# Attention passes of a graph network: each tile of neighbours gathered once, into 16 places, and copied from there step by step

## What is computed

```
# first: two GraphSAGE layers
agg = segment_sum(h[src], dst) * inv_deg          # mean over the incoming edges
h   = concatenate([h, agg]) @ W + b               # 128 -> 256, relu, 256 -> 128, log_softmax
# second: two attention layers (4 heads of 32)
k_j   = k[src] + e;  alpha = einsum(q[dst], k_j) / sqrt(32)      # e = edge weight * We
ex    = exp(alpha - segment_max(alpha, dst)[dst])
a     = ex / segment_sum(ex, dst)[dst]
out   = segment_sum((v[src] + e) * a, dst)
h     = relu(batchnorm(beta * x_r + (1 - beta) * out)) + h_res
```

## Time and profile before

| | us |
|---|---|
| median of 3 runs (8920.58 to 8937.23) | 8926.18 |
| profiled execution, its own time | 8917.18 |
| its span, first to last instruction | 8915.1 |
| first pass, first to last gather | 124.7 to 2075.7 |
| first attention pass, first to last gather | 4280.3 to 6377.2 |
| second attention pass, first to last gather | 6609.8 to 8705.1 |

### The profile page before, as it was taken

One profiled execution on the slowest core, in us unless ns is written; L12 is line 12 of the kernel. 1 busy time (PEld: TensorE's weight loads), 2 busy tenths in 40 slices (PEclk: granted clock), 3 DMA queues, 4 the chain that ended last, 5 costly groups with the idle time before them and its releaser, 6 DMA issues. The chain is left out here.

```text
span 8915.1 us, 117136 instructions
## 1 busy us (share of the span) xinstructions
PE 5021.9 (56%) x23604; PEld 4287.5 (48%) x23604; DVE 3720.9 (42%) x10693; ACT 3012.8 (34%) x10976; POOL 6457.3 (72%) x6755
## 2 busy tenths in 40 slices
PE   1444444446555555554666656666666666666666
PEld 1443443445444444443555555555455555555553
DVE  4000000003000000004677777777787777777778
ACT  4444444443433333333322222222222222222222
POOL 4777777773777777776677777777657777777776
PEclk7556556557555555556777777777787777777777
DMA  5333333336444444445666676766547667766663
GB/s 164 120 121 121 119 118 115 121 119 199 128 123 121 121 126 121 121 139 154 208 216 217 216 217 215 218 215 217 173 156 217 214 217 216 218 215 219 214 219 108
DMA packets 698550, 1514.21 MB, mean 170 GB/s; under 512 B 190785, under 2 KB 399706, under 8 KB 677966
## 3 DMA queue, kind: packets, MB, share of 16 engines
q0 software_dynamic: 258752, 639.99, 24.6%
q10 hardware_dynamic: 161312, 487.14, 15.8%
q1 hardware_dynamic: 277870, 380.19, 14.1%
HBM read 1294.45 MB, written 212.31 MB: 169 GB/s over the span
## 5 line engine op out<-in xcount | busy, mean ns | idle before, releaser
L1695 POOL DMA_INDIRECT conv_kv<-key_value,conv_src x3320 | 3183.3, 959 | 1100.0 <-issue 988.5
L881 POOL DMA_INDIRECT second_msg<-sage_hidden_projected,second_src x1516 | 1430.3, 943 | 585.4 <-issue 459.3
L881 POOL DMA_INDIRECT first_msg<-sage_in,first_src x1564 | 1475.6, 943 | 501.3 <-issue 476.1
L1933 PE MATMUL conv_ps_sums<-conv_kv,conv_sel 128*128 128x136 f32 x6640 | 1326.1, 352 | 584.4 <-DVE sums L1845 537.0
L2012 ACT ACTIVATE conv_selT<-conv_place,minus_partition 128x512 f32<-128x512 f32 x830 | 599.1, 722 | 2766.2 <-DVE conv_qwe L1737 2688.3
L1933 PEld LDWEIGHTS conv_ps_sums<-conv_kv,conv_sel 128*128 128x128 f32 x6640 | 1140.8, 246 | 729.2 <-DVE sums L1845 550.5
L1918 PE MATMUL conv_ps_query<-query_table,conv_selT 128*128 x6640 | 1245.4, 346 | 347.1 <-ACT conv_selT L2017 232.5
L1083 PE MATMUL first_ps_sums<-first_msg,first_sel 128*128 x3328 | 823.3, 431 | 1025.0 <-ACTq L951 994.9
L1918 PEld LDWEIGHTS conv_ps_query<-query_table,conv_selT 128*128 128x128 f32 x6640 | 1093.5, 246 | 436.5 <-issue 433.9
L1083 PE MATMUL second_ps_sums<-second_msg,second_sel 128*128 x3328 | 827.2, 429 | 786.7 <-ACTq L951 786.7
L1083 PEld LDWEIGHTS first_ps_sums<-first_msg,first_sel 128*128 128x128 f32 x3328 | 725.0, 322 | 1132.9 <-issue 1132.9
(11 more groups left out here) (271 smaller groups left out, 4229.8 us busy)
## 6 DMA issues: line engine op xcount, KB each, us to landing
conv_place<-place_rows SPq DMA_DIRECT2D x416, 512.0 KB
conv_sel<-selections ACTq DMA_DIRECT2D x414, 512.0 KB, 5.8
selections<-first_sel ACTq DMA_DIRECT2D x52, 2048.0 KB, 7.0
second_sel<-selections ACTq DMA_DIRECT2D x104, 1024.0 KB, 5.1
conv_kv<-key_value,conv_src POOLq DMA_INDIRECT x3320, 3.6
first_msg<-sage_in,first_src POOLq DMA_INDIRECT x1564, 2.5
second_msg<-sage_hidden_projected,second_src POOLq DMA_INDIRECT x1516
conv_pen<-run_penalties SPq DMA_DIRECT2D x416, 48.5 KB
```

Of the source, the lines that this page charges most:

```text
L881: pool.indirect_dma_start(msg[:, to * MW:to * MW + D], None, table, bass.IndirectOffsetOnAxis(ap=src[:, lap % 2, j:j + 1], axis=0)).then_i ...
L1695: pool.indirect_dma_start(kv[:, h * CH + j, :], None, t.kv_d, bass.IndirectOffsetOnAxis(ap=src[:, h, j:j + 1], axis=0)).then_inc(gathered[ ...
L1933: last = pe.matmul(sums_of(h, step), sel[:, k % SELG, step % GR, :], kv[:, h * CH + step, DEN:2 * D], start=True, stop=True)
```

## The change

- An attention pass gathers each tile once (391 groups of four), into `held`, a ring of 16 places. ScalarE copies a step's rows from there to the step's place in `kv` (56 places now), from an address in a register: for every half chunk it reads 16 places from a list, for every group the number of tile groups needed. VectorE waits for the copy (`copied`).
- SP loads the sources straight from the input, turns landed gathers into `tiles_in`, and frees a tile group (`held_free`) when the copies of its last step are done, two groups behind. All its other loads move to ScalarE's queue.
- The first pass also turns each selection: TensorE transposes it, ScalarE copies it out of PSUM (`keep_turned`) and a DMA of 256 KB a group stores it. The attention passes load turned selections two groups at a time; Abs, Relu and the broadcast rows go.
- Setup writes the two new lists and no longer the turned sources and place rows. The first own loads of both GraphSAGE passes are issued at the start of the pass (`begin`). The attention pass is unrolled on GpSimd and ScalarE, where it was a loop over pairs of chunks.

```
+HELD = 16
+HELD_GROUPS = HELD // GR
+LATE = 2
+PLACES = 56
+PLACE_GROUPS = PLACES // GR
...
 # first pass, ScalarE
+                def keep_turned(c, k):
+                    n = c * KG + k
+                    act.wait_ge(sel_turned, n + 1)
+                    if n >= 2:
+                        act.wait_ge(selT_out[n % 2], 16 * (n // 2))
+                    act.activation(selT[:, n % 2, :], psS[:, n % 2, :], ACT.Copy).then_inc(selT_taken, 1)
+                    act.wait_ge(selT_taken, n + 1)
+                    act.dma_start(t.selT_d[c, :, k * GR * P:(k + 1) * GR * P], selT[:, n % 2, :]).then_inc(selT_out[n % 2], 16)
...
                         release(n, h, g, k)
                         following(n + 1, 1 - h, g + h, k, used)
+                        if keeps and n + k > 0:
+                            keep_turned(*divmod(n * KG + k - 1, KG))
...
 # first pass, TensorE, behind the sums of each group
+                            for i in range(GR):
+                                last = pe.transpose(psS[:, n % 2, P * i:P * i + P], sel[:, h * CH + k * GR + i, :], t.ident[:, :])
+                            last.then_inc(sel_turned, 1)
...
 # attention pass, SP
+                def landed(g):
+                    sp.wait_ge(gathered[g % HELD_GROUPS], 16 * GR * (g // HELD_GROUPS) + 16 * GR)
+                    sp.sem_inc(tiles_in, 1)
+
+                def release(g):
+                    last = sp.value_load(lastuse[0:1, g:g + 1], min_val=1, max_val=STEPS // GR)
+                    sp.wait_ge(copied, last)
+                    sp.sem_inc(held_free, 1)
...
+                for g in range(GROUPS):
+                    landed(g)
+                    if g % KG == KG - 1 and (g // KG + 2) * CH < TILES:
+                        load_src(g // KG + 2)
+                    if g >= LATE and g - LATE + HELD_GROUPS < GROUPS:
+                        release(g - LATE)
...
 # attention pass, GpSimd
+                for g in range(GROUPS):
+                    lap, k = divmod(g, KG)
+                    if k == 0:
+                        pool.wait_ge(src_in[lap % 2], 16 * (lap // 2) + 16)
+                    if g >= HELD_GROUPS:
+                        pool.wait_ge(held_free, g - HELD_GROUPS + 1)
+                    pool.sem_inc(go_p, 1)
+                    for i in range(GR):
+                        j = k * GR + i
+                        pool.indirect_dma_start(
+                            held[:, (g * GR + i) % HELD, :], None, t.kv_d,
+                            bass.IndirectOffsetOnAxis(ap=src[:, lap % 2, j:j + 1], axis=0)).then_inc(gathered[g % HELD_GROUPS], 16)
...
 # VectorE
-                    dve.wait_ge(gathered[h * KG + k], 16 * GR * g + 16 * GR)
+                    dve.wait_ge(copied, KG * c + k + 1)
...
-                    mine = kv[:, h * CH:h * CH + CH, :]
-                    dve.tensor_copy(mine[:, :, DEN:DEN + HEADS], p)
+                    for lo, hi in runs_of(c):
+                        at_place = place_of_step(c * CH + lo)
+                        mine = kv[:, at_place:at_place + hi - lo, :]
+                        dve.tensor_copy(mine[:, :, DEN:DEN + HEADS], p[:, lo:hi, :])
...
 # ScalarE
+                def select_turned(a, q):
+                    c, h, g = a
+                    lo, hi = 2 * q, min(2 * q + 2, groups(a))
+                    half = q % (SELG // 2)
+                    act.wait_ge(q_ready, KG * c + 2 * q + SELG - 2)
+                    act.dma_start(selT[:, 2 * half:2 * half + hi - lo, :].rearrange("p k w -> p (k w)"),
...
+                def weights(c):
+                    act.wait_ge(wd_used, c + 1)
+                    act.dma_start(wd[:, c % 2, :, :], t.edge_d[:, 1:3, c * CH:c * CH + CH]).then_inc(wd_in[c % 2], 16)
+
+                def records(c):
+                    h = c % 2
+                    act.wait_ge(blk_used, c + 1)
...
+                def copy(a, k):
+                    c, h, g = a
+                    n = KG * c + k
+                    if k == 0:
+                        act.wait_ge(list_in[h], 16 * g + 16)
+                    if k % (KG // 2) == 0:
+                        regs = [act.alloc_register(f"{tag}_held{n}_{i}") for i in range(CH // 2)]
+                        act.load(regs, lists[0:1, h, k * GR:k * GR + CH // 2])
+                        from_tiles[:] = [act.snap(r, donate=True, min_val=0, max_val=HELD - 1) for r in regs]
+                    tiles = act.value_load(lists[0:1, h, CH + k:CH + k + 1], min_val=1, max_val=GROUPS)
+                    act.wait_ge(tiles_in, tiles)
+                    if n >= PLACE_GROUPS:
+                        act.wait_ge(sums_ready, 2 * KP + 2 * (n - PLACE_GROUPS) + 2)
+                    for i in range(GR):
+                        j = k * GR + i
+                        last = act.activation(kv[:, place_of_step(c * CH + j), :],
+                                              held[:, bass.ds(from_tiles[j % (CH // 2)], 1), :].rearrange("p a d -> p (a d)"), ACT.Copy)
+                    last.then_inc(copied, 1)
...
                     select(b, 0)
                     select(b, 1)
                     if a is not None:
-                        select_turned(a, 2)
+                        select_turned(a, 1)
+                        copy(a, 0)
                     act.wait_ge(drop_ready, c + 1)
                     act.activation(fac[:, :], drop[:, :], ACT.Exp).then_inc(fac_exp, 1)
                     act.wait_ge(below_ready, c + 1)
                     act.activation(expo[:, :], below[:, :], ACT.Exp).then_inc(expo_ready, 1)
                     if a is not None:
-                        for k in range(3, 6):
-                            select_turned(a, k)
+                        select_turned(a, 2)
+                        copy(a, 1)
+                        copy(a, 2)
+                        copy(a, 3)
+                    if after is not None:
+                        weights(after)
+                    if a is not None:
+                        select_turned(a, 3)
                     select(b, 2)
                     if a is not None:
-                        select_turned(a, 6)
+                        copy(a, 4)
+                        copy(a, 5)
                     select(b, 3)
+                    if after is not None:
+                        lists_of(after)
+                        records(after)
+                    if a is not None:
+                        copy(a, 6)
+                    if following is not None:
+                        select_turned(following, 0)
                     if a is not None and groups(a) == KG:
-                        select_turned(a, 7)
+                        copy(a, 7)
```

More of the change, by code:

```diff
@@ L256, in setup_phase @@
         bank = sb("bank", [SJ, P], I32)
+        held = sb("held", [SJ, P], I32)
         ring_f = sb("ring_f", [SJ, P])
@@ L688, in tensor, with begin @@
             last.then_inc(self.made, 1)
+    def begin(self, act):
+        self.load(act, (0, 0, 0))
+        self.load(act, (1, 1, 0))
+        act.wait_ge(self.w_in, 32)
     def load(self, act, turn):
@@ L766, in scalar @@
         n, h, g = turn
-        if isinstance(n, int) and n == 0:
-            self.load(act, (0, 0, 0))
-            self.load(act, (1, 1, 0))
         if not (isinstance(n, int) and n >= SPANS):
@@ L802, in sage_edges @@
         lastuse = sb("lastuse", [1, GROUPS], I32)
+        selT = sb("selT", [P, 2, GR * P]) if keeps else None
+        psS = psum("ps_sel", [P, 2, 512]) if keeps else None
+        sel_turned, selT_taken = sem("sel_turned"), sem("selT_taken")
+        selT_out = [sem(f"selT_out{b}") for b in range(2)]
         ps = psum("ps_sums", [P, SUM_BANKS * 512])
@@ L999, in pair @@
                         chunk(n, h, g, n - 1 if n > 0 else None)
+                own.begin(act)
                 if keeps:
@@ L1585, in slots_of, with place_of_step, runs_of, conv_edges @@
     return slots + [(last, ADDS[last - NEAR], CH, (PAIRS_OF[last - NEAR][0], KP))]
-def conv_edges(nc, t, tag):
+def place_of_step(step):
+    return step % PLACES
+def runs_of(c):
+    lo = place_of_step(c * CH)
+    return ((0, CH),) if lo + CH <= PLACES else ((0, PLACES - lo), (PLACES - lo, CH))
+def conv_edges(nc, t, src_cols, tag):
     with room(nc, tag) as (sb, psum, sem):
         HR = HEADS * CH
-        kv = sb("kv", [P, RING, 2 * D])
+        kv = sb("kv", [P, PLACES, 2 * D])
+        held = sb("held", [P, HELD, 2 * D])
+        lists = sb("lists", [1, 2, CH + KG], I32)
+        lastuse = sb("lastuse", [1, GROUPS], I32)
         sel = sb("sel", [P, SELG, GR, P])
         selT = sb("selT", [P, SELG, GR * P])
-        place = sb("place", [P, 2, 2 * GR * P])
         src = sb("src", [P, 2, CH], I32)
@@ L1685, in _ @@
             @block.gpsimd
             def _(pool):
-                def gathers(a):
-                    c, h, g = a
-                    pool.wait_ge(src_in[h], 16 * g + 16)
-                    for k in range(groups(a)):
```

(52 more changed lines are left out.)

132 lines of the change are left out of this document (57 added, 75 removed).

## The result

Median after the change 8872.33 us, beside 8921.71 for the kernel before in the same session: ratio 0.9944 [0.9933, 0.9956]. That is 49 us saved, where 171 were forecast. The profiled execution took 8870.64 us (span 8868.6) against 8917.18.

A forecast was written before the change was run, and what follows sets the result against it. POOL's gathers were taken to set the pace of all 104 stages. Stages 180 us saved, minus 7 for pass ends, minus 4 for the first pass's end, plus 2 for setup, made 171: median 8755 us, range 8680 to 8880.

The forecast's parts named there:

- The sixteen held places: Ring between POOL's gathers and ScalarE's copies: POOL can run on with 2.6 us in hand; 38.7 us a stage, 180 saved.
- the term of 0.3 for the coupling: Attention stage: loops of 38.1 and 38.4 us, so close, cost each other 0.3 us, giving 38.7.
- Landing: Held ring: a group is landed 3 x 1.25 + 3.6 = 7.4 us after its first gather starts.
- SP's serial release: SP frees a tile group behind the landing two groups later: 7.4 + 1.4 us, under POOL's 10.0.
- The copies' spread: ScalarE's copies against an even 4.75 us a group: offsets 3.6 to 0.4, spread 3.2, 2.6 us in hand.
- The ring is too short: Rival at `held_free`: POOL stops once a stage for up to 5.0 us; 43.1 a stage, 9200 us; chance 0.12.
- Gathers removed: POOL, attention passes: 1564 gathers instead of 1660 at 1.25 us, so 38.1 us a stage; that floor would give 242 us.
- Size of the copies: ScalarE, per group: four 128x256 copies replace Abs and Relu; 420 ns each, 1.4 us for four (bounds 1.28 and 2.5).
- The sixteen register reads: ScalarE, before the copies of groups 0 and 4: reading sixteen registers and a tile count takes 1.8 us.
- Group 0: VectorE waits 0.7 us for ScalarE's first copy of a stage (bounds 0 and 1.5).
- Group 1: VectorE waits 0.9 us for ScalarE's copy behind the exponential of `below` (bounds 0.3 and 1.5).
- Group 4: VectorE waits 0.7 us on average for ScalarE's copy, behind `select(b, 2)` and the register reads.

The follow-up runs named there:

- experiment 7: Changed kernel at sixteen held places, selection loads cut from 512 KB to 32 KB from the second chunk on: 8745.83 us; with SP also one group behind: 8738.89 us.
- experiments 6 and 9: 6: changed kernel with SP freeing one group behind, 8816.02 us. 9: 24 places, reads early, copies of groups 4 and 6 earlier, 8694.83; plus SP one behind, 8694.46.

## Why the prediction was wrong

**The failed step** is "The sixteen held places", which ends in "So POOL can run on, with 2.6 us in hand ... I take 0.3, so 38.7 us a stage". The loops on both sides of the ring came out as forecast: GpSimd 38.1 (measured 38.16 where nothing else bound), VectorE and ScalarE 38.4 (38.2 with half of the gathers). But the ring between them cost 1.8 us a stage, not 0.3. The stage was 40.0, not 38.7: 1.3 x 104 = 135 us, and the small terms below gave 11 back. The mechanism was on the list, its size was not: the term of 0.3 for the coupling is the one that failed. Three things in its budget were off:

- *Landing.* I took 3.6, a median over all places in a stage. Gathers at the end of a stage need 4.8 to their last packet alone, beside 2.8 to 3.1 elsewhere, and 5.8 until SP passed the group on in the stage shown. Shortening the loads gave 129 us over the change (experiment 7).
- *SP's serial release.* The budget compared 7.4 + 1.4 = 8.8 with 10.0 and called it enough. With 4.8 in place of 3.6 it is 10.0, and nothing is left; with the measured 5.8, 1.0 and 0.8 it is 3.75 + 7.5 = 11.3, and GpSimd stands 1.3 us, as it did before 5096.97. The cost of this order was 59 us at sixteen places and nothing at 24 (experiments 6 and 9).
- *The copies' spread.* The budget's own times put group 4 at 24, and 24 - 4 x 4.75 = 5.0; I wrote 3.6 as the largest offset. The right subtraction leaves 5.8 - (5.0 - 0.4) = 1.2 us in hand before any late landing, not 2.6. In the stage shown group 4 ended at 5075.1 - 5049.7 = 25.4, offset 6.4, and group 6 about 35, offset 6.7: over the 0.4 of group 2 that is 6.3, more than the window of 5.8.

Three quarters of the loss stood behind landings and a quarter behind copies (127 and 43 us), but the two hand over to each other when only one is mended. The prediction's rival "The ring is too short" had the place (`held_free`) and the ingredients (landing, SP's read, burst order) right and the price, up to 5.0 a stage, nearly three times too high. I had treated it as all or nothing; a window that is short by a little costs a little in every stage.

**The other steps.** Gathers removed: right, 1564 a pass at 1.25. Size of the copies: 403 ns against 420, four in 1.33 against 1.4. The sixteen register reads: from the end of the load's issue at 5072.01 to the copy at 5073.81, 1.80, as taken; the load of sixteen registers itself takes 1.03:

```profile
L2084 ACTq TENSOR_LOAD <-conv_lists x208: 1022/1034/1225, 4281.7 to 8653.6; - x104
```

The Trainium skill's 200 ns a register (Runtime: NRT & Kernel Launch, "Instruction fetch mechanics") would have been 3.2, an estimate from its figure, and this row does not bear it out. Group 0: 1.5 us on average, 2.46 in the stage shown; with half of the gathers, so that tiles have landed, 0.6 (0.7 forecast). Group 1: 2.48, of which 1.42 lie over VectorE's own register reads the earlier trace rows, so 1.1 against 0.9. Group 4: no wait for the copy (0.7 forecast); it waits for the queries, 0.9 on average, where the kernel before waited 0.8.

That VectorE's side came out at 38.2 against 38.4 is luck in part. Its 35.9 without gather waits was read from one stage. By the page it is 40.43 - (504.6 / 104 - 1.42) = 37.0, so the base was 1.1 too low; what the change added to it was 1.2, not 2.5. The two errors cancel.

The rest came out as follows. First pass: pace (2072.2 - 121.0)/1563 = 1.248 as forecast. Setup gave 3.7 us, forecast 2; the first pass's end cost 1.4, forecast 4 (the second pass starts gathering at 2197.9, before at 2200.2). Between there and the first softmax of the first attention pass 2.0 were lost, before that of the second pass 0.3, and 1.9 gained behind the last: 0.4 in all, against 7. These small terms came out 11 us better than taken, which hides part of the miss.

None of the prediction's own signs of being wrong came up. GpSimd's gaps over 0.30 stayed just under "2 us a stage" (1.97), a limit set too high for a coupling forecast at 0.3; the reads took less than 2.5; the first pass kept its pace.

## What to carry to other kernels

A ring between two engines that are equally fast is bought with slack, and the slack has to cover the latest landing and the latest copy of a stage, not the median of either: lay both out against an even pace, subtract for every group, and count anything serial between them (here SP's wait for a landing ahead of its release) as part of the round trip. When it is short, look for an order before a size: at the same sixteen places, three changes of order brought 151 of the 180 us that 24 places and the orders brought together. And changes to one loop need not add up; test them together before dropping one that alone gives little.

## What the runs showed of the hardware

TensorE's matmuls of the second and the first pass, groups by line of the changed kernel:

```profile
L1109 PE MATMUL second_ps_sums<-second_msg,second_sel 128*128 x3328 | 832.4, 430 | 794.4 <-ACTq L961 793.3 <-issue 0.9
...
L1109 PE MATMUL first_ps_sums<-first_msg,first_sel 128*128 x3328 | 712.3, 379 | 865.9 <-ACTq L961 865.1 <-issue 0.6
```

Engines' busy time in the changed kernel from 1000 to 1200 us, columns as in the earlier trace rows (PE, PEld, DVE, ACT, POOL, granted clock, DMA share, GB/s):

```profile
1000.00:1200.00 200.00, 115.22 (x541) 99.11 (x542) 4.59 (x20) 108.71 (x272) 151.23 (x161) 0.66 0.55 179
```

The change adds four transposes a group to the first pass, and the granted clock there went from 0.58 to 0.66, between the lower of its two levels (0.5, 1.2 GHz) and the upper (1.0, 2.4 GHz). The first pass's matmuls took 431 ns before and take 379 now; the second pass's, where nothing was added, 429 and 430. TensorE was given more to do there and does each piece quicker. It doesn't bind there, so the time shows nothing of it. The other surprise is in the table of landings: around three loads of 512 KB on another queue, within 1.3 us, a gather of 128 KB lands some 2 us later (4.8 against 2.8 to 3.1), and with loads of 32 KB it does not (2.5).
